# First attention of a two-layer block: two half-seen score blocks merged into one, and a new order of work

## What is computed

```python
q = (x @ wq).reshape(B, S, 32, 128)          # 32 query heads
k = (x @ wk).reshape(B, S, 8, 128)           # 8 key and value heads, each for 4 query heads
v = (x @ wv).reshape(B, S, 8, 128)
q, k = rope(q), rope(k)
scores = einsum('bqhgd,bshd->bhgqs', q, k) * 128 ** -0.5
allowed = (j <= i) & (j > i - 128)           # a row sees itself and the 127 rows before it
attn = softmax(where(allowed, scores, neg))
out = einsum('bhgqs,bshd->bqhgd', attn, v).reshape(B, S, 4096) @ wo
```

## Time and profile before

| what | value |
|---|---|
| median of three runs | 2203.28 us (2202.14 to 2205.8) |
| the profiled execution | 2204.66 us, of which the span is 2202.8 us |
| PE busy | 2151.4 us (98% of the span) |
| DVE busy | 1700.4 us (77%) |
| ACT busy | 1460.7 us (66%) |
| POOL busy | 1232.4 us (56%) |
| granted PE clock | 0.995 of full speed over the span |
| first attention | 64 gated outputs, from 78.8 to 737.2 us |

### The profile page before, as it was taken

The page is one execution under the profiler, slowest core; times in us unless marked ns, Lnnn a source line. Parts: engine busy times, 40 slices in busy tenths (PEclk is TensorE's granted clock), DMA queues, the critical chain, the costliest instruction groups (busy, mean ns, idle before and its releaser), DMA issues.

```text
span 2202.8 us, 41666 instructions
## 1 busy us (share of the span) xinstructions
PE 2151.4 (98%) x11084; PEld 1653.8 (75%) x11084; DVE 1700.4 (77%) x3415; ACT 1460.7 (66%) x2868; POOL 1232.4 (56%) x1091
## 2 busy tenths in 40 slices
PE   7999999999999999999999999999999999999988
PEld 5888888888887657777777777777777777777756
DVE  6777777777777668888888888888888877788865
ACT  3444444445444668888888888888888877777742
POOL 5656655665653446666666666666666620455334
PEclk9999999999999999999999999999999999999999
DMA  7011010010004142111111111111111111433341
GB/s 245 20 48 30 19 48 29 19 48 29 19 10 125 40 176 82 43 48 49 46 49 42 49 46 48 42 49 46 49 42 48 47 49 42 124 92 111 87 126 39
DMA packets 125422, 132.20 MB, mean 60 GB/s; under 512 B 33205, under 2 KB 75733, under 8 KB 125348
## 3 DMA queue, kind: packets, MB, share of 16 engines
q1 hardware_dynamic: 121508, 118.70, 18.1%
q0 software_dynamic: 3840, 12.59, 1.9%
HBM read 101.46 MB, written 29.10 MB: 59 GB/s over the span
## 4 chain that ended last, share of the span: by engine, by line
PE 92%; DVE 4%; ACT 1%; SPq 1%; issue 1%; POOL 0%; DMA 0%; DVEq 0%; ACTq 0%; POOLq 0%
PE bank L2464 12%; PE bank L2451 11%; PE bank L2471 11%; PE bank L2036 9%; PE bank L2038 9%; PE bank L2037 9%; PE bank L2492 6%; PE bank L2383 5%; PE bank L2382 5%; PE bank L2381 5%; PE bank L2489 2%; PE bank L2172 2%; DVE rope_b L1535 1%; DVE rope_b L1536 1%; DVE rope_a L1534 1%
## 5 line engine op out<-in xcount | busy, mean ns | idle before, releaser
L1817 DVE TENSOR_REDUCE mcol<-bank 128x1 fp32r<-128x512 f32 x1024 | 693.9, 689 | 221.6 <-PE bank L2451 211.2
L2464 PE MATMUL bank<-q,k 128*128 128x512 f32 x1024 | 418.8, 409 | 0.1
L2451 PE MATMUL bank<-km,q 128*128 128x512 f32 x1024 | 405.7, 397 | 2.9 <-DVE mcol L1817 1.6
L2471 PE MATMUL bank<-q,k 128*128 128x512 f32 x1024 | 406.2, 397 | 0.0
L2451 PEld LDWEIGHTS bank<-km,q 128*128 128x128 f32 x1024 | 316.2, 309 | 52.3 <-DVE mcol L1817 4.2
L1329 ACT ACTIVATE pT<-bank 128x512 f32<-128x512 f32 x512 | 284.5, 600 | 81.6 <-PE bank L2471 77.8
L1329 ACT ACTIVATE x<-bank 128x512 f32<-128x512 f32 x512 | 284.6, 600 | 80.8 <-PE bank L2471 77.0
L2464 PEld LDWEIGHTS bank<-q,k 128*128 128x128 f32 x1024 | 192.2, 188 | 127.0 <-ACT x L1329 44.3
L2471 PEld LDWEIGHTS bank<-q,k 128*128 128x128 f32 x1024 | 192.3, 188 | 32.4
L2383 PE MATMUL bank<-hT_hi,wr_lo 128*128 128x512 f32 x512 | 202.9, 396 | 0.0
L2381 PE MATMUL bank<-hT_hi,wr_hi 128*128 128x512 f32 x512 | 200.7, 392 | 1.6 <-DVE k L1690 1.6
(11 more groups left out here) (348 smaller groups left out, 5045.6 us busy)
## 6 DMA issues: line engine op xcount, KB each, us to landing
wst<-in_L_attn_Wq_rope SPq DMA_DIRECT2D x64, 256.0 KB, 3.0
o_d<-ost SPq DMA_DIRECT2D x504, 32.0 KB, 1.8
st_q<-in_L_attn_wq SPq DMA_DIRECT2D x8, 1024.0 KB, 7.4
st_wo<-in_L_attn_wo SPq DMA_DIRECT2D x8, 1024.0 KB, 5.2
km<-kc_d SPq DMA_DIRECT2D x256, 32.0 KB
q<-qc_d SPq DMA_DIRECT2D x256, 32.0 KB
k<-kc_d SPq DMA_DIRECT2D x256, 32.0 KB
wm<-in_L_wmod SPq DMA_DIRECT2D x6, 1024.0 KB, 9.3
```

The costliest lines, as they stand in the source:

```text
L1817: dve.tensor_reduce(mcol[:, k % 2, i % 4, i // 4:i // 4 + 1], bank[4 + i % 2][:], AX.X, ALU.max, negate=True)\
L2451: pe.matmul(bank[4 + i % 2][:], q2[:, k % 4, h, i % 4:S:4], km[:, b, h], start=True, stop=True).then_inc(max_mm, 1)
L2464: pe.matmul(bank[s % 4][:], k1[:, k % 2, t], q1[:, k % 4, h], start=True, stop=False)
L2471: pe.matmul(bank[s % 4][:], k2[:, k % 2, h, t], q2[:, k % 4, h], start=False, stop=True).then_inc(scores1, 1)
```

## The change

For the slots with `qb` above 0, the two blocks of scores become one. ACT copies the scores of the block before into `probs` (`scores_before`, two instructions of 2 x 128 columns). DVE overwrites, where the mask says so, with the scores of the own block (`copy_predicated`, two instructions), takes the row maximum over the merged block (`tensor_reduce`) and scales it (`tensor_scalar` on 128 x 4), each behind a wait for the one before. The exponentials, the normalising product, the turning and the high part then handle 128 columns for each head where they handled 256.

Since one merged and turned block now holds weights that belong to two value blocks, the sum over values is written as merged weights x values of the block before, plus (merged weights where they belong to the own block) x (own values - values of the block before). For this DVE makes the masked high part (a product with `own`), POOL the masked low part (`own_weights`, new), and the value differences are kept as `dv_hi` and `dv_lo`: the evacuation of Vt becomes three DVE instructions of 384 columns, and `dv_high` (ACT) and `dv_low` (DVE) are new, 384 columns each. `sum_values` keeps its six matmuls, the last three behind a second wait for POOL's part. The 0 and 1 triangle `own` is a new load of 64 KB at the start. The turned weights alternate between two PSUM banks.

The order of the items is new on all four engines. The core of the diff (left out are declarations, the first high split on ACT, the waits' new counts and the last head, where the same functions are called):

```diff
+            def own_weights(slot):
+                heads = lambda v: v.rearrange("p (h q) -> p h q", h=GQ)
+                mine = own[:].unsqueeze(1).broadcast_to([P, GQ, P])
+                pool.wait_ge(pT_split, 2 * slot + 1)
+                pool.tensor_tensor(heads(pT_lo[:, 1]), heads(pT_lo[:, 0].bitcast(F32)), mine, ALU.mult).then_inc(pT_split, 1)
...
+                    if split:
+                        split_weights(n + 1, (0,))
                     if b == 0:
                         split_wo(n)
                     if not (isinstance(n, int) and n == 0 and b == 0):
                         add_attention(4 * half - 1, TB * (1 - b) + 3)
                     rope_add(half + 1, "Q0", 1 - b)
-                    if split:
-                        split_weights(n + 1, (0,))
+                    own_weights(4 * half + 1)
                     rope_low(half + 1, "Q0", 1 - b)
                     rope(half + 1, "Q1", 1 - b)
                     rope(half + 1, "Q2", 1 - b)
+                    own_weights(4 * half + 2)
                     add_attention(4 * half, TB * b)
+                    if split:
...
+            def dv_high(half, b):
+                act.wait_ge(proj_free, TURNS * half + TURN["Vt"] + 1)
+                wait(act, pv0, 4 * half)
+                act.activation(dv_hi[:].rearrange("p t d -> p (t d)"), vT[:, 0:3 * P], ACT.Copy).then_inc(v_hi_done, 1)
+            def scores_before(slot, qb):
+                i = qb % 2
+                act.wait_ge(scores0, slot + 1)
+                for j in range(2):
+                    block = bank[j][:].rearrange("p (h k) -> p h k", h=2)[:, :, 0:P]
+                    act.activation(probs[:, i, 2 * j:2 * j + 2, 0:P], block, ACT.Copy).then_inc(masked0, 1)
             def exps(slot, qb):
...
-                c = slice(P, 2 * P) if qb == 0 else slice(0, 2 * P)
-                act.wait_ge(masked0, slot + 1)
+                c = slice(P, 2 * P) if qb == 0 else slice(0, P)
+                act.wait_ge(masked0, 5 * slot + 5)
...
-                    e = act.activation(probs[:, i, h, c], probs[:, i, h, c], ACT.Exp, bias=nmax[:, i, h:h + 1], scale=-1.0,
-                                       accum_out=den[:, i, h:h + 1])
+                    e = act.activation(probs[:, i, h, c], probs[:, i, h, c], ACT.Exp, bias=nmax[:, i, h:h + 1],
+                                       scale=-1.0 if qb == 0 else float(HD) ** -0.5, accum_out=den[:, i, h:h + 1])
...
+                    flat = lambda v: v.rearrange("p t d -> p (t d)")
+                    later = vT[:, 0:3 * P]
+                    dve.wait_ge(v_hi_done, 2 * half + 1)
+                    dve.tensor_tensor(flat(v_lo[:, b]), ps[:, 0:3 * P], flat(v_hi[:, b]).bitcast(F32), ALU.subtract)
+                    dve.tensor_tensor(later, ps[:, P:4 * P], flat(v_hi[:, b]).bitcast(F32), ALU.subtract).then_inc(kv_split, 1)
+                    dve.wait_ge(kv_split, 2 * half + 1)
+                    dve.tensor_tensor(later, later, flat(v_lo[:, b]).bitcast(F32), ALU.subtract).then_inc(proj_free, 1)
...
+            def dv_low(half, b):
+                dve.wait_ge(v_hi_done, 2 * half + 2)
+                dve.tensor_tensor(dv_lo[:].rearrange("p t d -> p (t d)"), vT[:, 0:3 * P],
+                                  dv_hi[:].rearrange("p t d -> p (t d)").bitcast(F32), ALU.subtract).then_inc(kv_split, 1)
             def mask(slot, qb):
...
-                c = slice(P, 2 * P) if qb == 0 else slice(0, 2 * P)
+                scale = float(HD) ** -0.5
                 dve.wait_ge(scores0, slot + 1)
                 dve.sem_inc(spare, 1)
-                for h in range(GQ):
-                    ps = bank[h // 2][:, (h % 2) * 2 * P:(h % 2 + 1) * 2 * P]
-                    e = dve.tensor_tensor_reduce(probs[:, i, h, c], ps[:, c], window[:, c], -(float(HD) ** -0.5), 3e38, ALU.add, ALU.min,
-                                                 nmax[:, i, h:h + 1])
...
+                block = lambda j, kb: bank[j][:].rearrange("p (h k) -> p h k", h=2)[:, :, kb * P:(kb + 1) * P]
+                seen = window[:, 0:P].bitcast(U32).unsqueeze(1).broadcast_to([P, 2, P])
+                dve.wait_ge(masked0, 5 * slot + 2)
+                dve.sem_inc(spare, 1)
+                for j in range(2):
+                    e = dve.copy_predicated(probs[:, i, 2 * j:2 * j + 2, 0:P], seen, block(j, 1))
                 e.then_inc(masked0, 1)
+                dve.wait_ge(masked0, 5 * slot + 3)
+                dve.tensor_reduce(nmax[:, i], probs[:, i, :, 0:P], AX.X, ALU.max, negate=True).then_inc(masked0, 1)
+                dve.wait_ge(masked0, 5 * slot + 4)
+                dve.tensor_scalar(nmax[:, i], nmax[:, i], scale, None, ALU.mult).then_inc(masked0, 1)
             def normalise(slot, qb):
...
+                c = slice(P, 2 * P) if qb == 0 else slice(0, P)
...
+                dve.tensor_tensor(probs[:, i, :, c], probs[:, i, :, c], rden[:, i].unsqueeze(2).broadcast_to([P, GQ, P]), ALU.mult)\
                    .then_inc(probs0, 1)
             def weights_low(slot, qb):
                 dve.wait_ge(pT_hi_done, slot + 1)
-                for kb in range(1 if qb == 0 else 0, 2):
-                    e = dve.tensor_tensor(pT_lo[:, kb], bank[2 + kb][:], pT_hi[:, kb].bitcast(F32), ALU.subtract)
-                e.then_inc(pT_split, 1)
+                if qb > 0:
+                    heads = lambda v: v.rearrange("p (h q) -> p h q", h=GQ)
+                    dve.tensor_tensor(heads(pT_hi[:, 1]), heads(bank[2 + qb % 2][:]), own[:].unsqueeze(1).broadcast_to([P, GQ, P]), ALU.mult)
+                dve.tensor_tensor(pT_lo[:, 0], bank[2 + qb % 2][:], pT_hi[:, 0].bitcast(F32), ALU.subtract)\
+                   .then_inc(pT_split, 2 if qb == 0 else 1)
...
                     mask(slot + 1, 1)
                     weights_low(slot, 0)
                     evacuate(half + 1, "Q0", nb)
+                    normalise(slot + 1, 1)
                     evacuate(half + 1, "Q1", nb)
+                    mask(slot + 2, 2)
                     out_low(slot)
-                    normalise(slot + 1, 1)
-                    mask(slot + 2, 2)
                     weights_low(slot + 1, 1)
+                    normalise(slot + 2, 2)
                     evacuate(half + 1, "Vt", nb)
-                    gate_attention(slot, b)
-                    normalise(slot + 2, 2)
-                    out_low(slot + 1)
                     evacuate(half + 1, "Q2", nb)
                     mask(slot + 3, 3)
+                    gate_attention(slot, b)
+                    out_low(slot + 1)
                     weights_low(slot + 2, 2)
+                    evacuate(half + 1, "Q3", nb)
                     normalise(slot + 3, 3)
-                    evacuate(half + 1, "Q3", nb)
                     out_low(slot + 2)
                     gate_attention(slot + 1, b)
...
                     if not last:
                         evacuate(half + 2, "K", b)
...
                     out_low(slot + 3)
+                    gate_attention(slot + 2, b)
+                    dv_low(half + 1, nb)
...
             def transposes(slot, qb):
...
-                for kb in range(1 if qb == 0 else 0, 2):
-                    for h in range(GQ):
-                        e = pe.transpose(bank[2 + kb][:, h * P:(h + 1) * P], probs[:, qb % 2, h, kb * P:(kb + 1) * P], ident[:])
...
+                c = slice(P, 2 * P) if qb == 0 else slice(0, P)
+                for h in range(GQ):
+                    e = pe.transpose(bank[2 + qb % 2][:, h * P:(h + 1) * P], probs[:, qb % 2, h, c], ident[:])
                 e.then_inc(trans0, 1)
             def sum_values(slot, half, b, qb):
...
-                mm3(bank[4][:], [(v_hi[:, b, qb - 1 + kb], v_lo[:, b, qb - 1 + kb], pT_hi[:, kb], pT_lo[:, kb])
-                                 for kb in range(1 if qb == 0 else 0, 2)], pv0)
+                at = max(qb - 1, 0)
+                pe.matmul(bank[4][:], v_hi[:, b, at], pT_hi[:, 0], start=True, stop=False)
+                pe.matmul(bank[4][:], v_hi[:, b, at], pT_lo[:, 0], start=False, stop=False)
+                e = pe.matmul(bank[4][:], v_lo[:, b, at], pT_hi[:, 0], start=False, stop=(qb == 0))
+                if qb > 0:
+                    pe.wait_ge(pT_split, 2 * slot + 2)
+                    pe.matmul(bank[4][:], dv_hi[:, at], pT_hi[:, 1], start=False, stop=False)
+                    pe.matmul(bank[4][:], dv_hi[:, at], pT_lo[:, 1], start=False, stop=False)
+                    e = pe.matmul(bank[4][:], dv_lo[:, at], pT_hi[:, 1], start=False, stop=True)
+                e.then_inc(pv0, 1)
...
                     scores(slot + 1, half, b, 1)
                     transposes(slot, 0)
                     project(half + 1, "Q0", nb, n + b)
+                    project(half + 1, "Q1", nb, n + b)
+                    scores(slot + 2, half, b, 2)
+                    project(half + 1, "Vt", nb, n + b)
+                    transposes(slot + 1, 1)
                     sum_values(slot, half, b, 0)
```

(9 more changed lines are left out.)

119 lines of the change are left out of this document (70 added, 49 removed).

## The result

The changed kernel takes 2226.86 us (median of 4 runs, 2224.35 to 2227.45) against 2204.54 us for the kernel before (4 runs, 2202.14 to 2205.89). The ratio is 1.010, its 95% interval 1.0083 to 1.0118: slower by 22.3 us, where 10 were forecast.

What follows compares the result with a forecast made beforehand. PE was taken as the bound, DVE next. A half of 42.10 us, less 0.49 and 1.32, plus 2.37 of waits, is 42.66: 9.0 us over 16 halves, plus 1.1 in the prologue, gave 2213 us, range 2196 to 2230.

Steps and rivals of the forecast that it cites:

- The sum for a half of the first attention: Half of a head in the first attention: 42.10 less 0.49, less 1.32, plus 2.37 makes 42.66 us.
- What PE saves: Turned blocks on PE: three slots drop 4 of 8, 1.32 us a half; best case a half of 40.3 us.
- DVE's string by work alone fits: DVE from Q0's evacuation to the second slot's low part: 16.0 us of work, under the 16.7 that PE leaves.
- The unit costs: DVE's mask instructions in the trace: predicated copies about 0.42 us, maxima 0.69 unstretched by POOL, scalings 0.17 to 1.3.
- the fourth rival: DVE's predicated copy takes two passes, 0.61 us instead of 0.34, 17 us more: 2230; chance 0.06.
- Product collisions: DVE's normalising products wait for POOL: about 1.6 us behind Q0's evacuation and pT_lo, up to 2.6 beside wo_lo, 0.69 undisturbed.
- The scaling meets POOL: DVE's 128 x 4 scaling waits for POOL's rope add of Q2: bounds 0 and 1.15 us, 0.75 taken.
- the second rival: Collisions cost less, as the scaling does not meet POOL: a half of 41.9 us, 2201 in all; chance 0.20.
- PE's waits, 2.05 and 2.7 us: PE waits for DVE 2.05 us in a head's second half, 2.7 in its first: turned blocks, Q2, project_out(slot + 1).
- The prologue, 1.1 us: Before the first half, Vt's longer evacuation and dv_low delay Q2 and Q3 on DVE; PE waits 1.1 us.
- the list of edits that cost nothing: Claimed free: ACT's two copies of 256 columns, POOL's 3.9 us more a half, the load of own.
- the faster one: At most 0.7 us of collisions in DVE's string: a half of 40.3 to 41.8 us, about 2178 at best; chance 0.22.

Runs made afterwards that it cites:

- on_act_128: Changed kernel with DVE's scaling of the maxima and normalising products of slots 1 to 3 on ACT, allocations back on multiples of 128 bytes: 2183.20 us.
- on_act: Changed kernel with the scaling of the row maxima and the normalising products of slots 1 to 3 moved from DVE to ACT: 2193.94 us.
- no_scale: Changed kernel without DVE's scaling of the row maxima, so that factor of the softmax is left out: 2208.05 us.
- after_128: Changed kernel with only the allocations of nmax and den moved, so what follows lies on multiples of 128 bytes again: 2219.13 us.
- before_256: Kernel before with cT, silu_e, silu_d, nmax and den moved to the end of the first layer's tensors, the others 256 bytes lower: 2205.59 us.
- dv_low_late: after_128 with DVE's dv_low(0, 0) in the prologue moved behind the evacuations of Q2 and Q3: 2218.94 us.
- place_before: Kernel before with only the allocations of cT, silu_e and silu_d moved, nearly all tensors behind them 192 bytes lower: 2219.04 us.
- no_own: Changed kernel without POOL's product for the masked low part, which is left out of the computation: 2205.10 us.
- old_order: after_128 with the merged blocks in the item order of the kernel before on all four engines: 2296.99 us.
- norm_behind_q1: Changed kernel with DVE's normalising product of the first masked slot moved from behind Q0's evacuation to behind Q1's: 2217.46 us.

## Why the prediction came out as it did

The direction and the mechanism were right: DVE's waits for POOL reach PE and eat more than the turned blocks save. The sum for a half of the first attention came within 0.02 us, once the placement is out, and that closeness is in part luck, since two errors of 0.2 us cancel (below). The total was 13.9 us short: 9.3 for a cost that I had not looked for, some 3 for the prologue and 1 for the last head.

- **What PE saves**: right, a little more than said. Without waits a half is 40.05 us (on_act_128) where the forecast had 40.28.
- **DVE's string by work alone fits**: right as far as rows can say. It is 18.85 us with and 15.9 without its collisions, where the forecast gave it 16.7. No kernel ran with all of DVE's work and no collision; on_act, where PE waits for nothing although ACT has 4 us more a half, has also less work on DVE.
- **The unit costs**: the predicated copy took 0.43 to 0.46 us and a pair 0.78, near the forecast's 0.42 (one pass, which closes the fourth rival); the maximum 0.69, never stretched; the scaling 0.17 free and up to 1.10.
- **Product collisions**: behind Q0's evacuation 1.68 us, and 2.52 beside `wo_lo` (forecast 1.6 and up to 2.6), behind `pT_lo` 1.77 (forecast 1.6).
- **The scaling meets POOL**: right, and it is what separated the forecast from the second rival: no_scale is worth 1.16 us a half where its work alone gives 0.6. The forecast had 0.75 us for it, and it is 0.91. The Trainium skill (page "SBUF — State Buffer", section "Who interferes with whom") has `tensor_scalar` among the instructions that can take the shared pair and `tensor_reduce` among those that never do; the trace agrees with both, 1.10 us for 4 columns against 0.69 for 512 beside the same POOL work. It also says that the loser blocks for the whole instruction; the product beside `wo_lo` began its 0.69 us of work 0.15 us before that had ended, so nearly. And it says that ACT waits for nobody; on_act agrees, where each of the 192 activations that took the place of products took 385 to 405 ns beside the same POOL work.
- **PE's waits, 2.05 and 2.7 us**: the idle time is less, 1.37 and 2.03, and it fell on the three places named, though never on `gated`. But a wait costs more than its idle time: the starts of two matmuls, 0.23 us apart without a wait, are 0.86 us apart around the wait of 0.46 at 290.84, and the first one behind it takes 0.50 us instead of 0.39. Between after_128 and the half without waits the loss is 2.16 and 3.01 us. I had 2.37 for the mean of both and it is 2.59; the 0.22 more and the 0.23 that PE saved more cancel.
- **The prologue, 1.1 us**: mis-sized and put on the wrong instruction. Between before_256 and after_128 the first output projection moved by 4.0 us (73.72 to 77.70). These are single executions: that of before has it at 75.63, which would leave 2.1, so the cost is known to some 2 us only. `dv_low` is not the cause (dv_low_late). The rows name POOL's `bq_lo` for `scores(0)` (1.65 us against 0.50) and ACT's copies for the first mask (2.84 us of DVE's time); ACT has two activations for the gate ahead of them (L1049 in the changed kernel), which wait 1.41 us for PE; the forecast had said that a mask would start later by what ACT is late, and had not looked at the prologue for it. That was only read from the trace, not tried, and the cause stays open.
- **The last head**: its half became 1.5 us longer (47.06 to 48.53), where I had counted it as any other: 1 us too little.
- **What failed**: the list of edits that cost nothing. The moved allocation of `cT`, `silu_e` and `silu_d` stood in the diff and I gave it no term. It is worth 13.1 us on the kernel before (place_before), 10.7 on on_act, and on the change 9.3 (22.3 less 13.0), where a half grew by 0.2 us only; that PE's waits absorb the rest there fits, but was not tried by itself.

The rival with a free scaling (2201) and the faster one (2178 at best) both needed fewer collisions than this order has. The kernels that take some or most of them away come near those times, no_scale with 2208.1, no_own with 2205.1 and on_act_128 with 2183.2, but none of them is just the rival's case.

## What to carry to other kernels

When work moves to DVE, read for each instruction what POOL is doing at that moment, not DVE's total: 4 columns of a scaling cost as much as a full instruction if they meet one. A place right behind the instruction that releases POOL is a bad one for an instruction with two SBUF operands (1.68 to 2.52 us for 0.69 here); on ACT, or one step later, it cost less. An allocation that moves is a part of the change: shift what lies behind it by a multiple of 128 bytes, the only one of four shifts that was free here, or time the move by itself. And a kernel that PE bounds is lost in small pieces that no view of waits shows, so compare distances between the same instructions too.

## What the runs showed of the hardware that I had not expected

- **The pace of 128x512 matmuls depends a little on where tensors lie in SBUF.** Shifting nearly all tensors down by 32, 64, 192 and 256 bytes from multiples of 128 changed a half of 42.07 us by 0.41, 0.23, 0.40 and 0.00, and the whole kernel by 0.43%, 0.27%, 0.65% and nothing. Single groups went from 390 to 394 or from 396 to 401 ns, without a wait, while others kept their pace. The kernel with the 192-byte shift also spread more than the others (2213.6 to 2225.1 us over 6 runs, against 2203.3 to 2206.5 over 11 for 256 bytes); why is open.
- **A short wait of PE can cost as much again behind it**: after a wait of 1.92 us PE's granted clock was 0.50 for six microseconds in one execution of the prologue (dv_low_late), and in old_order it was 0.57 over the 4 us behind waits of 2.43 and 2.83 us. Half the clock for six microseconds is three lost, more than the wait; 0.57 over four is 1.7, less than it. Behind the waits of 1.42 and 1.71 us in norm_behind_q1, and of 1.65 us in the prologue of after_128, it stayed at 1.00.
- **A predicated copy costs one pass**: 0.44 us for 256 columns with a PSUM source and a broadcast mask from SBUF, where a step of the old mask took 0.41 for as many, and POOL doesn't stretch it (0.46 at most, over 96 of them).
